# A gated state-space block with a BitNet feed-forward on one core: seven roundings move from GpSimd to VectorE, with a new order of all four queues

## The chip, the cores and the metric

One core of a Trainium2 chip. The time is the device time of one execution in microseconds (us). In the profile PE is TensorE (PEld its weight load), DVE VectorE, ACT ScalarE, POOL GpSimd, SP the engine that issues DMAs.

## The reference

Four batches (B = 4) of 256 tokens with 256 channels. What is computed:

```
z = layernorm(x); h = ctx @ in_proj.T; u = silu(causal conv, 4 taps, of h)
dt_lo, Bm, Cm = u @ x_proj.T            (8, 16 and 16 rows)
delta = softplus(dt_proj @ dt_lo + b);  A = -exp(A_log)
state = state * exp(delta * A) + (delta * u) * Bm    (over 256 steps, 16 states)
y = (sum over states of state * Cm + D * u) * silu(z)
x = x + tanh(g_xattn) * y
n = layernorm(x)
gate, up = act_quant(n) @ weight_quant(w_gate).T, the same with w_up     (256 -> 1024)
i = silu(gate) * up
x = x + tanh(g_ffn) * act_quant(fwht(i)) @ weight_quant(w_down).T        (1024 -> 256)

act_quant(v) = clip(round(v * s), -128, 127) / s,  s = 128 / max|v| of the token
weight_quant(w): w / mean|w| rounded and clipped to -1, 0, 1
fwht: normalized fast Walsh-Hadamard transform over the 1024 channels
```

## The kernel before

Each engine has a list of pieces, written out by hand in the order in which it works them off; between engines stand semaphores alone. A piece waits for its inputs at its head, and whatever is behind it in the same list waits too. Since all four batches are in flight at once, the place of a piece in its list decides much.

The state-space part of a batch f is cut into eight steps of two states; step g = 8f + j. For each: `decays(g)` (ScalarE: four exponentials), `drives(g)` (GpSimd: four products, token on the partition), `drive_rows(g, h)` (TensorE: transposes into PSUM, one bank for each half h), `scan(g, 0)` and `scan(g, 1)` (VectorE: the recurrence), `C_rows(g)` (TensorE), `times_C(g)` (VectorE), `accumulate(g)` (TensorE: sum over the states, transposed back). Rings tie them: decays(g) wait for scan(g-4), drives(g) for drive_rows(g-4), drive_rows(g, h) for scan(g-1, h). The drives of steps 0 and 1 are made by VectorE.

Ahead of it, for each batch: in_proj, silu_u, x_dbl, dt_rows, high_pieces and split (the rows of B and C in bf16 pieces), dt_proj, softplus with softplus_tail on GpSimd, du_T and copy_duT.

Behind it, for each batch f: residual, stats2 (VectorE), rstd2 (ScalarE), second_rstd (GpSimd, eight instructions of one column), second_norm (ScalarE), token_scale (VectorE), scale_tokens (ScalarE: times the scale, plus a magic number), then the **token rounding** (take the magic number off, min with 127, into bf16), tokens_T (TensorE), tokens_out. For each half of the tokens t: gate, silu_gate, up, gate_times_up (VectorE), three fold stages of two instructions each (GpSimd for batches 0 to 2, VectorE's fold_last for batch 3), inter_T, inter_out, hadamard_mm, absmax2 (VectorE), quant_down (ScalarE), the **down rounding** of a 128 x 1024 tile, q2_T, q2_out, down, result (VectorE) and the store. The intermediate lies in `wnat`, the rounded down tile in `wq`, what quant_down writes in `ctxs`.

The two roundings are one instruction each, `tensor_scalar(..., MAGIC + QB - 1, MAGIC, min, subtract)`. In the kernel before GpSimd makes them for tokens of batches 0, 1, 2 (`round_tokens_early`, L1294) and for down tiles (0,0), (0,1), (1,0), (1,1) (`round_down_early`, L1298); VectorE makes those of tokens of batch 3 (L1593) and of down tiles (2,0) to (3,1) (L1632). quant_down waits for the down rounding before it, since both use `ctxs`. gate(f, 0) waits for quant_down(f-1, 1), whose bank it takes.

At the front, ctx_out copies the transposed context of batches 1 to 3 that in_proj(1) needs; weight_abs, weight_sum, weight_means, weight_scale, weight_round, weight_T and weight_out make the ternary weights, spread over batches 0 and 1.

Of the kernel before, what the change touches and what calls it, by code (L numbers as in the profile page):

```python
# [17 lines left out]
LC = L // P  # L18
# [34 lines left out]
def gated_ssm_ffn(nc, x, ctx_1024, g_xattn, g_ffn, in_proj_w, conv_w, conv_b, x_proj_w, dt_proj_w, dt_proj_b,  # L53
                  A_log, D, w_gate, w_up, w_down, ident, hadamard, out):
    stack = ExitStack()
    with stack:
# [3 lines left out]
        def sem(name):  # L60
# [146 lines left out]
        dve_stat2, act_r2, rounded, pe_qT, dve_qT, pe_gate, pe_up, act_sg, dve_mul, act_qT, act_q2T = (  # L207
            sem(n) for n in ("dve_stat2", "act_r2", "rounded", "pe_qT", "dve_qT", "pe_gate", "pe_up", "act_sg", "dve_mul",
                          "act_qT", "act_q2T"))
        pool_fold, pe_tp, act_tp, pe_h, dve_sc, act_tq, rounded_down, pe_q2T, dve_q2T, pe_dn, dve_out = (  # L210
            sem(n) for n in ("pool_fold", "pe_tp", "act_tp", "pe_h", "dve_sc", "act_tq", "rounded_down", "pe_q2T", "dve_q2T",
# [117 lines left out]
        def _(pe):  # L329
# [220 lines left out]
            def tokens_T(f):  # L550

                pe.wait_ge(rounded, f + 1)
# [86 lines left out]
            def q2_T(f, t):  # L639
                pe.wait_ge(rounded_down, LC * f + t + 1)  # L640
# [56 lines left out]
            setup_late()  # L697
# [3 lines left out]
            B_rows(0)  # L701
            in_proj(1, 0)
            du_T(0)
            B_rows(1)
            C_rows(0)
            in_proj(1, 1)
            x_dbl(1)
            drive_rows(2, 0)
            C_rows(1)
            drive_rows(2, 1)  # L710
            dt_proj(1)
            drive_rows(3, 0)
            accumulate(0)
            drive_rows(3, 1)
            C_rows(2)
            drive_rows(4, 0)
            gate_T(0)
            accumulate(1)
            C_rows(3)
            drive_rows(4, 1)  # L720
            drive_rows(5, 0)
            in_proj(2, 0)
            drive_rows(5, 1)
            C_rows(4)
            weight_sum()
            accumulate(2)
            drive_rows(6, 0)
            C_rows(5)
            accumulate(3)
            drive_rows(6, 1)  # L730
            du_T(1)
            accumulate(4)
            in_proj(2, 1)
            C_rows(6)
            weight_T(0)
            drive_rows(7, 0)
            drive_rows(7, 1)
            x_dbl(2)
            drive_rows(8, 0)
            weight_T(1)  # L740
            accumulate(5)
            drive_rows(8, 1)
            accumulate(6)
            C_rows(7)
            drive_rows(9, 0)
            drive_rows(9, 1)
            C_rows(8)
            dt_proj(2)
            accumulate(7)
            drive_rows(10, 0)  # L750
            gate_T(1)
            C_rows(9)
            drive_rows(10, 1)
            weight_T(2)
            drive_rows(11, 0)
            accumulate(8)
            in_proj(3, 0)
            drive_rows(11, 1)
            accumulate(9)
            C_rows(10)  # L760
            drive_rows(12, 0)
            in_proj(3, 1)
            drive_rows(12, 1)
            accumulate(10)
            weight_T(3)
            weight_T(4)
            du_T(2)
            C_rows(11)
            drive_rows(13, 0)
            weight_T(5)  # L770
            x_dbl(3)
            C_rows(12)
            drive_rows(13, 1)
            tokens_T(0)
            accumulate(11)
            gate(0, 0)
            drive_rows(14, 0)
            drive_rows(14, 1)
            C_rows(13)
            gate(0, 1)  # L780
            drive_rows(15, 0)
            drive_rows(15, 1)
            up(0, 0)
            C_rows(14)
            up(0, 1)
            drive_rows(16, 0)
            drive_rows(16, 1)
            accumulate(12)
            C_rows(15)
            drive_rows(17, 0)  # L790
            accumulate(13)
            drive_rows(17, 1)
            accumulate(14)
            dt_proj(3)
            drive_rows(18, 0)
            C_rows(16)
            accumulate(15)
            C_rows(17)
            drive_rows(18, 1)
            accumulate(16)  # L800
            inter_T(0, 0)
            drive_rows(19, 0)
            C_rows(18)
            drive_rows(19, 1)
            drive_rows(20, 0)
            hadamard_mm(0, 0)
            drive_rows(20, 1)
            accumulate(17)
            inter_T(0, 1)
            drive_rows(21, 0)  # L810
            C_rows(19)
            gate_T(2)
            C_rows(20)
            drive_rows(21, 1)
            hadamard_mm(0, 1)
            accumulate(18)
            drive_rows(22, 0)
            drive_rows(22, 1)
            q2_T(0, 0)
            C_rows(21)  # L820
            tokens_T(1)
            accumulate(19)
            du_T(3)
            gate(1, 0)
            drive_rows(23, 0)
            drive_rows(23, 1)
            gate(1, 1)
            accumulate(20)
            drive_rows(24, 0)
            up(1, 0)  # L830
            drive_rows(24, 1)
            C_rows(22)
            accumulate(21)
            down(0, 0)
            accumulate(22)
            q2_T(0, 1)
            C_rows(23)
            drive_rows(25, 0)
            up(1, 1)
            drive_rows(25, 1)  # L840
            accumulate(23)
            gate_T(3)
            C_rows(24)
            down(0, 1)
            drive_rows(26, 0)
            C_rows(25)
            drive_rows(26, 1)
            drive_rows(27, 0)
            inter_T(1, 0)
            hadamard_mm(1, 0)  # L850
            drive_rows(27, 1)
            C_rows(26)
            accumulate(24)
            inter_T(1, 1)
            drive_rows(28, 0)
            accumulate(25)
            hadamard_mm(1, 1)
            q2_T(1, 0)
            accumulate(26)
            C_rows(27)  # L860
            drive_rows(28, 1)
# [1016 lines left out]
```

## Time and profile before

| what | us |
|---|---|
| median of 3 runs | 239.27 (238.29 to 240.78) |
| the profiled execution | 238.49 |
| its span in the trace | 236.4 |
| busy PE / DVE / ACT / POOL | 177.0 / 185.4 / 165.5 / 168.6 |

The span is from the first to the last instruction in the trace; the time of an execution has some us around it. Busy times are sums over the span, and no engine is busy throughout; what bounds a stretch has to be read from that stretch.

### The profile page before, as it was taken

The numbers are of one execution on the slowest core, as the hardware profiler recorded it, in microseconds if no ns is written. First come the engines' busy times: TensorE is split into PE (matmuls) and PEld (weight loads), VectorE is DVE, ScalarE is ACT, GpSimd is POOL, SyncE is SP. The second block draws the span as 40 slices with busy tenths as digits, with TensorE's granted clock in tenths as the row PEclk, the third lists the DMA queues.
The fourth block names the chain that finished last, engine by engine and source line by source line (L and its number), as shares of the span: only waits on it lengthen the run. The fifth ranks groups of instructions, "written<-read, shape, count | busy, mean of one in ns | idle before, by whom it ended". The sixth has DMA issues, their size and how long they took to land.

```text
span 236.4 us, 3708 instructions
## 1 busy us (share of the span) xinstructions
PE 177.0 (75%) x1216; PEld 144.1 (61%) x1216; DVE 185.4 (78%) x270; ACT 165.5 (70%) x285; POOL 168.6 (71%) x262
## 2 busy tenths in 40 slices
PE   3876859988987977788778599956746987575864
PEld 2545637977866966476677467745633776433752
DVE  3518986799999996999978946997668885579962
ACT  2499999996999983999956479968445614733230
POOL 1003079996799999999999999999999999500000
PEclk9985575599999999999979979999999999998895
DMA  3795000000000000000000000000000000000001
GB/s 65 224 348 217 1 1 0 4 0 0 3 0 3 0 0 4 0 0 1 3 1 0 0 0 3 22 25 1 0 0 3 24 22 3 0 22 0 3 22 44
DMA packets 8148, 6.33 MB, mean 27 GB/s; under 512 B 2202, under 2 KB 7874, under 8 KB 8130
## 3 DMA queue, kind: packets, MB, share of 16 engines
q1 hardware_dynamic: 7154, 6.02, 8.0%
q10 hardware_dynamic: 976, 0.09, 0.3%
q8 instruction: 10, 0.16, 0.3%
q14 instruction: 8, 0.07, 0.1%
HBM read 5.05 MB, written 1.05 MB: 26 GB/s over the span
## 4 chain that ended last, share of the span: by engine, by line
POOL 41%; ACT 21%; PE 15%; issue 9%; DVE 8%; DMA 3%; SPq 1%; POOLq 0%; DVEq 0%; ACTq 0%
POOL driveT L1276 11%; POOL wnat L1340 9%; POOL wnat L1341 9%; ACT decay L983 7%; POOL wq L1298 5%; DMA ctxs<-in_ctx_dram 3%; PE PY L468 2%; PE GP L598 2%; POOL q L1294 2%; DVE wnat L1604 2%; DVE wnat L1615 2%; ACT wq L1098 2%; DVE wnat L1614 1%; PE X L497 1%; PE BC L407 1%
## 5 line engine op out<-in xcount | busy, mean ns | idle before, releaser
L1276 POOL TENSOR_SCALAR driveT<-duT,BT 128x256 f32<-128x256 f32 x120 | 56.9, 500 | 13.7 <-ACT duT L1000 10.9
L983 ACT ACTIVATE decay<-delta,zero_c,aneg 128x255 f32<-128x255 f32 x128 | 64.9, 588 | 0.8 <-DVE state L1478 0.7
L1478 DVE TENSOR_TENSOR_SCAN state<-decay,BC 128x512 f32<-128x512 f32 x30 | 36.4, 1213 | 9.8 <-issue 6.9
L1478 DVE TENSOR_TENSOR_SCAN state<-decay,UP 128x512 f32<-128x512 f32 x30 | 36.1, 1203 | 5.7 <-issue 3.3
L1555 DVE TENSOR_TENSOR prod<-state,BC 128x1024 f32<-128x1024 f32 x32 | 38.3, 1198 | 1.1 <-DVE state L1478 0.8
L468 PE MATMUL PY<-id,prod 128*128 128x128 f32 x256 | 35.5, 284 | 1.4 <-DVE prod L1555 0.9
L468 PEld LDWEIGHTS PY<-id,prod 128*128 128x128 f32 x256 | 30.5, 147 | 3.0 <-DVE prod L1555 1.6
L1340 POOL TENSOR_TENSOR wnat<-wnat 128x512 f32<-128x512 f32 x18 | 22.9, 1274 | 0.9 <-DVE wnat L1604 0.2
L1341 POOL TENSOR_TENSOR wnat<-wnat 128x512 f32<-128x512 f32 x18 | 22.9, 1274 | 0.0
L1102 ACT COPY hT<-GP 128x1024 f32<-128x1024 f32 x8 | 8.1, 1008 | 21.2 <-PE GP L616 21.2
L407 PE MATMUL BC<-id,driveT 128*128 128x128 f32 x120 | 19.8, 291 | 3.2 <-POOL driveT L1276 2.2
L407 PE MATMUL UP<-id,driveT 128*128 128x128 f32 x120 | 19.3, 286 | 0.8 <-DVE state L1478 0.7
L407 PEld LDWEIGHTS BC<-id,driveT 128*128 128x128 f32 x120 | 14.8, 150 | 6.4 <-POOL driveT L1276 2.7
L598 PE MATMUL GP<-wT,qT 128*128 128x512 bf16 x56 | 14.6, 383 | 5.0 <-ACT wq L1098 2.8
L407 PEld LDWEIGHTS UP<-id,driveT 128*128 128x128 f32 x120 | 15.3, 149 | 2.9 <-issue 1.7
L452 PE MATMUL BC<-bc,sel 96*128 96x256 bf16 x64 | 13.0, 285 | 5.3 <-DVE prod L1555 5.3
L616 PE MATMUL GP<-id,wnat 128*128 128x128 f32 x64 | 9.0, 286 | 7.6 <-POOL wnat L1341 3.4
L1305 POOL TENSOR_TENSOR rest<-raw,high 64x256 f32<-64x256 f32 x4 | 2.7, 665 | 16.7 <-ACT raw L1041 16.7
L1298 POOL TENSOR_SCALAR wq<-ctxs 128x1024 bf16<-128x1024 f32 x4 | 14.6, 3639 | 0.0
L616 PEld LDWEIGHTS GP<-id,wnat 128*128 128x128 f32 x64 | 7.3, 145 | 8.9 <-POOL wnat L1341 3.8
L1098 ACT ACTIVATE wq<-GP,zero_c,gs 128x1024 f32<-128x1024 f32 x7 | 8.4, 1205 | 5.9 <-PE GP L598 5.9
L1604 DVE SCALAR_TENSOR_TENSOR wnat<-GP,us,wq 128x1024 f32<-128x1024 f32 x7 | 8.9, 1271 | 3.6 <-issue 2.9
(210 smaller groups left out, 390.5 us busy)
## 6 DMA issues: line engine op xcount, KB each, us to landing
wnat<-in_L_ffn_w_gate_dram SPq DMA_DIRECT2D x1, 1024.0 KB, 9.4
xs<-in_x_dram SPq DMA_DIRECT2D x1, 1024.0 KB, 11.8
wnat<-in_L_ffn_w_up_dram SPq DMA_DIRECT2D x1, 1024.0 KB, 11.9
wnat<-in_L_ffn_w_down_dram SPq DMA_DIRECT2D x1, 1024.0 KB, 11.3
out_dram<-ot SPq DMA_DIRECT2D x8, 128.0 KB, 1.7
ctxs<-in_ctx_dram SPq DMA_DIRECT2D x1, 384.0 KB, 6.9
ctxs<-in_ctx_dram SPq DMA_DIRECT2D x1, 128.0 KB, 2.7
inw<-n_L_xattn_in_proj_w_dram SPq DMA_DIRECT2D x1, 128.0 KB, 2.7
```

Source lines behind the costliest of these rows:

```text
L407: last = nc.tensor.transpose(drive_bank(h)[:, L * n + P * c:L * n + P * (c + 1)], driveT[:, m % RING, c, n, P * h:P * (h + 1)], id32[:])
L468: last = nc.tensor.matmul(PY[:, E * c + P * h:E * c + P * (h + 1)], prod[:, g % RING, h, n, P * c:P * (c + 1)], id32[:], is_transpose=True ...
L598: last = nc.tensor.matmul(ffn_bank(f, t)[:, 512 * i:512 * (i + 1)], qT[:, h, P * t:P * (t + 1)], w[:, h, 512 * i:512 * (i + 1)], start=(h ...
L616: last = nc.tensor.transpose(GP[:, P * a:P * (a + 1)], fold[:, t, P * a:P * (a + 1)], id32[:])
L983: last = nc.scalar.activation(decay[:, m % RING, h, n, 1:L], delta[:, b % 2, h, 1:L], ACT.Exp, bias=zero_c[:], scale=aneg[:, h, NB * j + n ...
L1276: last = nc.gpsimd.tensor_scalar(driveT[:, m % RING, c, n], duT[:, b % 2, c], BT[:, b % 2, c, NB * j + n:NB * j + n + 1], 1.0, ALU.mult, A ...
L1298: nc.gpsimd.tensor_scalar(q2[:, t], tq, MAGIC + QB - 1, MAGIC, ALU.min, ALU.subtract).then_inc(rounded_down, 1)
L1340: nc.gpsimd.tensor_tensor(dst[:, :, 0, :], src[:, :, 0, :], src[:, :, 1, :], ALU.add)
L1341: nc.gpsimd.tensor_tensor(dst[:, :, 1, :], src[:, :, 0, :], src[:, :, 1, :], ALU.subtract).then_inc(done, 1)
L1478: nc.vector.tensor_tensor_scan(state[:, g % STATES, h].rearrange("p n l -> p (n l)"), decay[:, g % RING, h].rearrange("p n l -> p (n l)"), ...
L1555: nc.vector.tensor_tensor(prod[:, g % RING].rearrange("p h n l -> p h (n l)"), state[:, g % STATES].rearrange("p h n l -> p h (n l)"), PC. ...
L1604: nc.vector.scalar_tensor_tensor(out=inter[:, t], in0=ffn_bank(f, t)[:], scalar=us[:, t:t + 1], in1=sg[:, t], op0=ALU.mult, op1=ALU.mult). ...
```

## The change

All seven roundings that GpSimd made go to VectorE; `round_tokens_early` and `round_down_early` are gone, and the semaphores are renamed. VectorE's list has `round_tokens(0)` before times_C(12), `round_down(0, 0)` before scan(20, 0), `round_tokens(1)` between scan(21, 0) and result(0, 0), `round_down(0, 1)` before times_C(20), `round_down(1, 0)` before times_C(26), `round_tokens(2)` after scan(28, 0), `round_down(1, 1)` after scan(30, 0). The lists of all four engines are put in a new order throughout; no piece but the roundings changes its engine, and no instruction changes.

The core of the diff (order lists shortened to the places that matter here):

```diff
@@ GpSimd
-            def round_tokens_early(f):
-                pool.wait_ge(act_xr, f + 1)
-                nc.gpsimd.tensor_scalar(q[:], xn[:], MAGIC + QB - 1, MAGIC, ALU.min, ALU.subtract).then_inc(rounded, 1)
-
-            def round_down_early(f, t):
-                pool.wait_ge(act_tq, LC * f + t + 1)
-                nc.gpsimd.tensor_scalar(q2[:, t], tq, MAGIC + QB - 1, MAGIC, ALU.min, ALU.subtract).then_inc(rounded_down, 1)
...
             token_factors(0)
-            drives(14)
-            drives(15)
-            round_tokens_early(0)
-            drives(16)
             drives(17)
...
             drives(22)
-            round_down_early(0, 0)
-            softplus_tail(3, pool, nc.gpsimd, pool_front_link, 1)
-            round_tokens_early(1)
-            token_factors(1)
             softplus_tail(3, pool, nc.gpsimd, pool_front_link, 2)
             drives(23)
             drives(24)
             drives(25)
-            round_down_early(0, 1)
             drives(26)
             fold_tile(1, 0, 0)
             fold_tile(1, 0, 1)
+            drives(27)
             fold_tile(1, 0, 2)
-            drives(27)
             fold_tile(1, 1, 0)
             fold_tile(1, 1, 1)
-            drives(28)
             fold_tile(1, 1, 2)
             second_rstd(2)
-            round_down_early(1, 0)
+            drives(28)
+            token_factors(2)
             drives(29)
-            round_tokens_early(2)
-            token_factors(2)
             drives(30)
             drives(31)
-            round_down_early(1, 1)
             fold_tile(2, 0, 0)
@@ VectorE
             def round_tokens(f):
                 dve.wait_ge(act_xr, f + 1)
-                nc.vector.tensor_scalar(q[:], xn[:], MAGIC + QB - 1, MAGIC, ALU.min, ALU.subtract).then_inc(rounded, 1)
+                nc.vector.tensor_scalar(q[:], xn[:], MAGIC + QB - 1, MAGIC, ALU.min, ALU.subtract).then_inc(dve_q, 1)
...
+            round_down(0, 0)
             scan(20, 0)
             scan(20, 1)
             times_C(19)
             token_scale(1, dve_ln_link)
             scan(21, 0)
+            round_tokens(1)
+            result(0, 0)
+            absmax2(0, 1)
             scan(21, 1)
+            round_down(0, 1)
             times_C(20)
-            absmax2(0, 1)
...
             scan(27, 0)
             scan(27, 1)
+            round_down(1, 0)
             times_C(26)
+            token_scale(2, dve_ln_link)
             scan(28, 0)
-            token_scale(2, dve_ln_link)
+            round_tokens(2)
             absmax2(1, 1)
...
             scan(30, 0)
+            round_down(1, 1)
             gate_times_up(2, 0)
-            result(1, 0)
             scan(30, 1)
-            gate_times_up(2, 1)
             times_C(29)
             scan(31, 0)
             scan(31, 1)
+            result(1, 0)
             times_C(30)
+            gate_times_up(2, 1)
+            times_C(31)
             result(1, 1)
-            times_C(31)
...
             tokens_out(3)
+            absmax2(2, 1)
             q2_out(2, 0)
-            absmax2(2, 1)
+            gate_times_up(3, 0)
+            round_down(2, 1)
+            fold_last(0)
+            gate_times_up(3, 1)
             result(2, 0)
-            gate_times_up(3, 0)
-            fold_last(0)
-            round_down(2, 1)
-            gate_times_up(3, 1)
             fold_last(1)
@@ ScalarE
+            silu_u(0)
             inw_out()
-            tanh_gates()
-            silu_u(0)
-            ctx_out()
             for_exp()
             dt_rows(0)
+            high_pieces(0)
             weight_abs(0)
+            softplus(0)
             exp_A()
-            high_pieces(0)
-            softplus(0)
             copy_B(0)
+            ctx_out()
             copy_BT(0)
...
             decays(3)
-            copy_BT(1)
-            high_pieces(1)
+            softplus(1)
             decays(4)
-            softplus(1)
+            gate_out(0)
+            weight_abs(2)
             decays(5)
-            weight_abs(2)
-            gate_out(0)
             decays(6)
...
+            q2_out_early(1, 0)
+            tokens_out_early(2)
             quant_down(1, 1)
-            tokens_out_early(2)
             silu_gate(2, 0)
             silu_gate(2, 1)
-            q2_out_early(1, 0)
@@ TensorE
             gate(3, 0)
+            gate(3, 1)
+            up(3, 0)
             down(2, 0)
-            up(3, 0)
-            gate(3, 1)
             up(3, 1)
```

## Rows read from the trace of the kernel before

**Rows 1.** Busy time of each engine by stretch (x instructions), granted clock, DMA:

```profile
core 0: us, PE busy (x) PEld busy (x) DVE busy (x) ACT busy (x) POOL busy (x), PEclk, DMA share, GB/s
30.00:60.00 30.00, 25.31 (x145) 22.14 (x146) 24.30 (x25) 27.70 (x53) 25.44 (x37) 0.77 0.01 2
60.00:90.00 30.00, 25.46 (x210) 22.46 (x209) 29.67 (x37) 27.75 (x56) 28.29 (x54) 1.00 0.00 1
90.00:185.00 95.00, 70.79 (x536) 57.77 (x536) 77.60 (x94) 70.02 (x116) 93.20 (x129) 0.96 0.01 4
185.00:203.00 18.00, 13.89 (x117) 11.88 (x115) 13.10 (x20) 6.92 (x10) 17.06 (x21) 1.00 0.05 16
203.00:236.40 33.40, 20.84 (x148) 15.07 (x147) 23.71 (x44) 11.17 (x12) 1.76 (x5) 0.86 0.05 16
```

**Rows 2.** Chain of waits that ended last, share of the span by engine:

```profile
POOL 41%; ACT 21%; PE 15%; issue 9%; DVE 8%; DMA 3%; SPq 1%; POOLq 0%; DVEq 0%; ACTq 0%
```

**Rows 3.** Groups of instructions by shape, GpSimd: the roundings:

```profile
L1298 POOL TENSOR_SCALAR wq<-ctxs 128x1024 bf16<-128x1024 f32 x4 | 14.6, 3639 | 0.0
...
L1294 POOL TENSOR_SCALAR q<-xn 128x512 bf16<-128x512 f32 x3 | 5.8, 1935 | 0.0
```

**Rows 4.** Groups by shape, VectorE: the same roundings in the tail:

```profile
L1632 DVE TENSOR_SCALAR wq<-ctxs 128x1024 bf16<-128x1024 f32 x4 | 2.8, 692 | 1.3 <-ACT ctxs L1108 1.3
...
L1593 DVE TENSOR_SCALAR q<-xn 128x512 bf16<-128x512 f32 x1 | 0.4, 428 | 0.5 <-ACT xn L1092 0.5
```

**Rows 5.** Timeline, GpSimd (start, duration): pairs beside roundings, one alone:

```profile
77.27 1.60 POOL L1320 TENSOR_SCALAR nt<-ve,r 128x1 f32<-128x1 f32 x2
...
123.51 0.50 POOL L1320 TENSOR_SCALAR nt<-ve,r 128x1 f32<-128x1 f32 x2
...
205.21 1.04 POOL L1287 TENSOR_SCALAR gs<-amax,wmean 128x1 f32<-128x1 f32 x2 [2.19 <-DVE amax L1585]
206.21 0.74 POOL L1289 TENSOR_SCALAR us<-amax,wmean 128x1 f32<-128x1 f32 x2
```

**Rows 6.** Timeline, VectorE, at the same times:

```profile
77.28 1.22 DVE L1656 TENSOR_SCALAR wq<-wnat 128x2048 bf16<-128x2048 f32 x1
...
205.27 0.69 DVE L1632 TENSOR_SCALAR wq<-ctxs 128x1024 bf16<-128x1024 f32 x1
206.47 0.43 DVE L1593 TENSOR_SCALAR q<-xn 128x512 bf16<-128x512 f32 x1 [0.51 <-ACT xn L1092]
```

**Rows 7.** Timeline, GpSimd: drives of batch 3, folds of batch 2:

```profile
137.29 5.64 POOL L1276 TENSOR_SCALAR driveT<-duT,BT 128x256 f32<-128x256 f32 x12
...
185.28 1.27 POOL L1340 TENSOR_TENSOR wnat<-wnat 128x512 f32<-128x512 f32 x1 [0.20 <-DVE wnat L1604]
...
199.29 1.27 POOL L1341 TENSOR_TENSOR wnat<-wnat 128x512 f32<-128x512 f32 x1
```

**Rows 8.** Timeline, VectorE: times_C(6), times_C(14), gaps, gate_times_up(1,0), gate_times_up(2,0):

```profile
63.26 1.19 DVE L1555 TENSOR_TENSOR prod<-state,BC 128x1024 f32<-128x1024 f32 x1
...
101.74 1.20 DVE L1555 TENSOR_TENSOR prod<-state,BC 128x1024 f32<-128x1024 f32 x1
...
140.02 1.22 DVE L1478 TENSOR_TENSOR_SCAN state<-decay,BC 128x512 f32<-128x512 f32 x1 [3.32 <-issue]
...
144.32 1.28 DVE L1604 SCALAR_TENSOR_TENSOR wnat<-GP,us,wq 128x1024 f32<-128x1024 f32 x1 [1.98 <-issue]
...
183.91 1.28 DVE L1604 SCALAR_TENSOR_TENSOR wnat<-GP,us,wq 128x1024 f32<-128x1024 f32 x1 [0.68 <-PE GP L598]
```

**Rows 9.** Timeline, ScalarE: decays(5) and second_norm(3):

```profile
45.03 2.06 ACT L983 ACTIVATE decay<-delta,zero_c,aneg 128x255 f32<-128x255 f32 x4
...
203.05 1.09 ACT L1084 ACTIVATE xn<-x,mr,rn 128x256 f32<-128x256 f32 x2 [0.29 <-POOL mr L1326]
```

**Rows 10.** Groups by shape, ScalarE: the decays:

```profile
L983 ACT ACTIVATE decay<-delta,zero_c,aneg 128x255 f32<-128x255 f32 x128 | 64.9, 588 | 0.8 <-DVE state L1478 0.7
```

More of the change, by code:

```diff
@@ L770, in _ @@
+            accumulate(11)
+            C_rows(12)
+            drive_rows(13, 1)
+            du_T(2)
             weight_T(5)
             x_dbl(3)
[L772 to L776, printed above, removed]
             drive_rows(14, 0)
             drive_rows(14, 1)
+            tokens_T(0)
+            gate(0, 0)
             C_rows(13)
+            drive_rows(15, 0)
             gate(0, 1)
[L781 removed]
@@ L798, in _ @@
+            dt_proj(3)
+            drive_rows(16, 1)
+            C_rows(15)
+            accumulate(14)
+            drive_rows(17, 0)
+            drive_rows(17, 1)
+            accumulate(15)
+            C_rows(16)
+            drive_rows(18, 0)
+            up(0, 1)
+            drive_rows(18, 1)
+            inter_T(0, 0)
             C_rows(17)
-            drive_rows(18, 1)
+            hadamard_mm(0, 0)
+            drive_rows(19, 0)
+            gate_T(2)
+            drive_rows(19, 1)
@@ L813, in _ @@
+            drive_rows(21, 1)
+            tokens_T(1)
+            drive_rows(22, 0)
+            accumulate(19)
             C_rows(20)
[L814 to L817, printed above, removed]
             drive_rows(22, 1)
-            q2_T(0, 0)
+            gate(1, 0)
+            accumulate(20)
+            du_T(3)
+            drive_rows(23, 0)
             C_rows(21)
-            tokens_T(1)
-            accumulate(19)
-            du_T(3)
@@ L824, in _ @@
-            gate(1, 0)
-            drive_rows(23, 0)
+            gate(1, 1)
             drive_rows(23, 1)
-            gate(1, 1)
-            accumulate(20)
+            up(1, 0)
+            accumulate(21)
+            C_rows(22)
             drive_rows(24, 0)
-            up(1, 0)
+            C_rows(23)
             drive_rows(24, 1)
-            C_rows(22)
-            accumulate(21)
-            down(0, 0)
+            q2_T(0, 1)
+            drive_rows(25, 0)
             accumulate(22)
-            q2_T(0, 1)
@@ L837, in _ @@
-            C_rows(23)
-            drive_rows(25, 0)
+            drive_rows(25, 1)
+            C_rows(24)
             up(1, 1)
-            drive_rows(25, 1)
+            drive_rows(26, 0)
+            down(0, 1)
             accumulate(23)
-            gate_T(3)
[L843 to L847, printed above, removed]
+            inter_T(1, 0)
+            drive_rows(26, 1)
+            C_rows(25)
+            hadamard_mm(1, 0)
@@ L1202, in _ @@
             decays(18)
+            softplus(3)
             decays(19)
+            inter_out(0, 0)
             decays(20)
+            gate_out(2)
+            quant_down(0, 0)
+            rstd2(1)
             decays(21)
-            softplus(3)
             decays(22)
-            inter_out(0, 0)
-            decays(23)
-            rstd2(1)
-            quant_down(0, 0)
+            q2_out_early(0, 0)
             second_norm(1)
@@ L1214, in _ @@
             scale_tokens(1)
-            gate_out(2)
+            decays(23)
+            tokens_out_early(1)
+            quant_down(0, 1)
             for_silu()
             silu_z(3)
-            tokens_out_early(1)
-            quant_down(0, 1)
+            silu_gate(1, 0)
             copy_duT(3)
-            silu_gate(1, 0)
-            q2_out_early(0, 0)
             silu_gate(1, 1)
@@ L1731, in _ @@
             times_C(10)
+            scan(12, 0)
             weight_out(2)
+            scan(12, 1)
+            times_C(11)
             token_scale(0, dve_ln_link)
-            scan(12, 0)
-            scan(12, 1)
             weight_out(3)
-            weight_out(4)
-            times_C(11)
-            weight_out(5)
             scan(13, 0)
             scan(13, 1)
+            weight_out(4)
+            weight_out(5)
+            round_tokens(0)
             times_C(12)
```

238 lines of the change are left out of this document (116 added, 122 removed).

## Prediction

> **What bounds the kernel now.** I read the busy time by stretch first, because averages hide the stages. Four stretches differ [rows 1]. In 30 to 60 us no engine is full, ScalarE is nearest (27.70 of 30). In 60 to 90 VectorE is full (29.67 of 30). In 90 to 185 GpSimd is (93.20 of 95), while VectorE has 17.4 us free, ScalarE 25.0, TensorE 24.2. From 203 on GpSimd does 1.76 us and the last batch runs as one dependent chain of 33.4 us. Then the chain of waits: 41% of it lies on GpSimd, ScalarE is next with 21% [rows 2]. Then GpSimd's own groups by tile: the roundings are seven instructions, four of 3639 ns for the down tiles (L1298) and three of 1935 ns for tokens (L1294), 14.6 + 5.8 = 20.4 us [rows 3], all inside 90 to 185. So what bounds the middle is GpSimd, with these in its queue; there the end is set by gate_times_up(2,0) on VectorE (183.91), behind which GpSimd folds without a gap (185.28 to 200.56) before it can make the statistics of the last batch [rows 7, 8].
>
> **The roundings.** VectorE makes the same two instructions for the last tiles already: 692 ns and 428 ns [rows 4]. GpSimd loses 20.4 us, VectorE gains 4 x 0.69 + 3 x 0.43 = 4.1 us. Two bounds of the gain follow: GpSimd alone could give 20.4; VectorE has 17.4 us free in 90 to 185 and takes 4.1, so at most 13.3 us can go before VectorE is full there. From below: zero, if each rounding on VectorE waits as long as it saves.
>
> Each rounding also takes its wait with it. On VectorE scans and times_C stand behind it, and ScalarE (next decays), TensorE (drive_rows wait for scans) and GpSimd (drives wait for drive_rows) behind those. The wait is for ScalarE (scale_tokens, quant_down), whose own queue has groups of four decays in it at 588 ns each [rows 10], 2.1 us as pitched.
>
> **The order.** I laid the new lists of the four busy engines end to end with durations of the old trace, each piece starting at the latest of its waits. The landmarks:
> - Front. ctx_out now follows softplus(0), so in_proj(1) and with it x_dbl(1) come later; softplus(1), gate_out(0) and weight_abs(2) stand before decays(5), which begins near 50.1 instead of 45.03 [rows 9]. It costs little, since VectorE's queue was later than that already: I get the end of times_C(6) near 64.8 plus a weight_out that was inside the old figure, against 63.26 + 1.19 = 64.5 [rows 8], so 1.0 us late. Drives of GpSimd begin 2 us earlier, but wait for duT(1), near 61.9, as before. The full stretch 60 to 90 hands the 1.0 us on. Round_tokens(0) waits for scale_tokens(0), which ends near 91.9, VectorE being there at 92.3: no wait. The gaps of 90 to 103 take the lateness up: times_C(14) ends near 102.8, against 101.74 + 1.20 = 102.9 [rows 8]. Gain so far 0. Bounds: 5 us worse if decays(5) shifts the scans in full, 2 us better if the earlier drives are passed on.
> - Batch 1. Its tokens are rounded near 128.7 rather than on GpSimd at 135.1. What is late next is quant_down(0,1) near 132.1 (gate(1,0) waits for its bank), behind absmax2(0,1), and then the copy of duT(3), near 136.5; in the old trace the last eight of the twelve drives at 137.29 stood behind it [rows 7]. The idle 3.32 and 1.98 us of VectorE at 140 and 144 [rows 8] shrink: gate_times_up(1,0) starts near 140.0, old 144.32. Gain 4.3.
> - Batch 2. GpSimd now runs from 141.2 through six fold stages (twelve instructions of 1.27), drives(27) and second_rstd(2) without a rounding, to 161.1. Then come second_norm(2), token_scale(2), round_tokens(2) near 165.3, absmax2(1,1), quant_down(1,1) near 168.8, gate(2,0), silu, gate(2,1), silu, up(2,0); gate_times_up(2,0) starts near 175.0, old 183.91. Gain 8.9. GpSimd stands idle near 170 to 176: it has stopped being the bound there, and the loop VectorE, ScalarE, TensorE is.
> - Folds of batch 2. Twelve instructions, 15.3 us as before (185.28 to 199.29 + 1.27) [rows 7], gate_times_up(2,1) being in time near 183.8; then second_rstd(3). second_norm(3) near 193.7, old 203.05 [rows 9]. Gain 9.4.
> - Tail. The same chain of 33.4 us [rows 1]. gate(3,1) ahead of up(3,0) and an early absmax2(2,1) hide nothing that was late, but result(2,0) leaves a gap of VectorE and now stands between gate_times_up(3,1) and fold_last(1): its 0.4 us and some placing, +0.4. Bounds -1 and +1.5.
>
> Sum of the lists: 236.4 - 9.4 + 0.4 = 227.4 us of span.
>
> **A cost the lists don't have.** Some of GpSimd's instructions stretch when VectorE rounds. The pair L1320 takes 0.50 us at 123.51 but 1.60 at 77.27, exactly while a weight rounding of 1.22 runs on VectorE (77.28). At 205.21 the pair gs takes 1.04 instead of 0.50, beside round_down(2,0) at 205.27; at 206.21 the pair us takes 0.74, beside q at 206.47 [rows 5, 6]. So GpSimd stands still for 0.54 us at a down rounding and 0.24 at a token rounding; 4 x 0.54 + 3 x 0.24 = 2.9 us for the seven, bounded by 0 and by the 4.1 us that they run. Half of GpSimd's time in question is on the path (it idles near 136 and 170), so +1.5. Span 228.9.
> The Trainium skill (SBUF - State Buffer, "Who interferes with whom") says that VectorE and GpSimd share one pair of ports by an exclusive lock, and that a VectorE instruction in a two-port mode shuts GpSimd out while it runs; the trace agrees, with the 1.60 against 0.50 us. By its full lock the cost would be the upper bound, 4.1, and not 2.9.
>
> **The time.** The profiled execution took 238.49 us with a span of 236.4, so 2.1 us lie around it: 228.9 + 2.1 = 231.0. The median of the runs, 239.27, is 0.8 above that execution: 231.8.
>
> **Rivals.**
> - *VectorE waits for GpSimd.* The stand-still could also go the other way: a rounding that finds a fold instruction of 1.27 us running waits for its end, half of it on average, 7 x 0.64 = 4.4 us, and the waiting is on VectorE, which is then the engine of the loop. With the other 1.4 us of the stand-still also on the path: 231.8 + 5.8 = 237.6. For it: fold instructions fill much of 141 to 161. Against it: no rounding or weight rounding of the old trace shows a wait before it; but none met a long instruction of GpSimd as it began. The page named above says that whichever instruction starts first keeps the pair, which is this rival's rule.
> - *The roundings are queued too early on VectorE.* Place: round_down(0,0), round_tokens(1), round_down(0,1), round_tokens(2). If ScalarE's piece before them is one group of decays late, scans stand for 2.07 us, the decays behind wait for the scans, and nothing catches up. All seven: 231.8 + 14.5 = 246.3. It turns slower by over 1% from (241.7 - 231.8) / 7 = 1.4 us of waiting per rounding. For it: at round_down(0,1) my lists leave no slack (quant_down ends 132.1, VectorE is there at 132.1). Against it: in the others VectorE comes 0.5 to 3 us after the data.
> - *The full bound.* My list is too strict in the loop (old waits hold some overlap that I charge twice), and VectorE fills up in 90 to 185: 239.3 - 13.3 = 226.0. For it: the earlier drives. Against it: four engines in a loop have never all been full in the old trace.
>
> **Chances.** Forecast 231.8 (228.5 to 235.5): 0.68. VectorE waits for GpSimd, 237.6: 0.13. Too early, 246.3: 0.08. Full bound, 226: 0.11. The range for 8 in 10 is 226.5 to 238.0, the second rival in, the third mostly out. A run of this kernel can tell about 1% (its three times span 238.3 to 240.8). Faster by over 1% (under 236.9): the forecast, the full bound and a small part of the first rival, 0.81; within 1%: 0.11; slower: 0.08.
>
> **What would show it.** In the changed profile: no L1298 or L1294 on GpSimd, seven more short ones on VectorE with less than 0.5 us of idle before each; GpSimd idle for some us before the folds of batch 2; gate_times_up(1,0) near 140 and gate_times_up(2,0) near 175; the tail still 33 us. Pairs such as gs that stretch beside a rounding confirm the stand-still. Wrong would be: times_C(14) well after 103 (the front costs), gate_times_up(2,0) after 181 (the gain is lost in the loop), or idle of over 1.4 us before each rounding.

## The result and the profile after

Median after 235.21 us (234.16 to 236.20, four runs), before on the same chip 239.17 (238.29 to 240.78): ratio 0.985 [0.980, 0.989]. A second measurement on another chip gave 0.982 [0.978, 0.985]. So the change is 1.5 to 1.8% faster, some 4 us, where 231.8, a gain of 7.5, was forecast; the range 226.5 to 238.0 holds the time. The profiled execution took 235.95 us, with a span of 234.2 and a mean granted clock of 0.934.

Busy time by stretch, the changed kernel:

```profile
core 0: us, PE busy (x) PEld busy (x) DVE busy (x) ACT busy (x) POOL busy (x), PEclk, DMA share, GB/s
30.00:60.00 30.00, 23.15 (x123) 19.43 (x124) 23.45 (x24) 26.55 (x50) 26.27 (x36) 0.77 0.00 1
60.00:90.00 30.00, 27.89 (x220) 24.74 (x218) 29.75 (x36) 26.30 (x56) 25.91 (x47) 0.94 0.00 1
90.00:185.00 95.00, 73.93 (x581) 60.56 (x580) 89.12 (x109) 75.52 (x124) 81.50 (x134) 0.98 0.01 4
```

Against [rows 1], GpSimd has fallen from 93.20 to 81.50 us of 95 and VectorE has risen from 77.60 to 89.12: no engine is full in the middle any more. The chain of waits says the same; before it was 41% GpSimd and 8% VectorE [rows 2]:

```profile
POOL 33%; ACT 22%; PE 22%; DVE 12%; issue 9%; DMA 1%; SPq 0%; POOLq 0%; ACTq 0%; DVEq 0%
```

The landmarks of the prediction, from the timelines (us). "After" is the first profile of the changed kernel and "after, again" a second one, from experiment 6; "drive_rows late" is experiment 10, the changed kernel with one piece of TensorE moved back:

| landmark | before | forecast | after | after, again | drive_rows late |
|---|---|---|---|---|---|
| end of times_C(6) | 64.5 | 64.8 | 66.1 | 65.6 | 62.8 |
| end of times_C(14) | 102.9 | 102.8 | 105.8 | 104.5 | 101.7 |
| gate_times_up(1,0) starts | 144.3 | 140.0 | 143.7 | 142.7 | 139.6 |
| gate_times_up(2,0) starts | 183.9 | 175.0 | 179.8 | 178.8 | 176.1 |
| second_norm(3) starts | 203.1 | 193.7 | 198.9 | 197.9 | 195.2 |
| from there to the end of the span | 33.4 | 33.7 | 35.3 | 33.4 | 34.2 |

Stretch by stretch the span changed by +2.9 (front), -3.5 (to gate_times_up(1,0)), -3.5 (to gate_times_up(2,0)), 0 (folds) and +2.0 (tail) in the first profile, 2.2 us less together; in the second by +1.5, -3.1, -3.5, 0 and 0, 5.1 less. The medians differ by 4: the first profiled execution of after was 0.7 us slower than its median, that of before 0.7 to 0.8 faster.

VectorE, changed kernel, the rows that answer to [rows 8], and second_norm(3) of ScalarE, to [rows 9]:

```profile
104.62 1.21 DVE L1540 TENSOR_TENSOR prod<-state,BC 128x1024 f32<-128x1024 f32 x1
...
143.71 1.26 DVE L1589 SCALAR_TENSOR_TENSOR wnat<-GP,us,wq 128x1024 f32<-128x1024 f32 x1
...
179.78 1.28 DVE L1589 SCALAR_TENSOR_TENSOR wnat<-GP,us,wq 128x1024 f32<-128x1024 f32 x1 [0.58 <-issue]
```

```profile
198.90 1.09 ACT L1084 ACTIVATE xn<-x,mr,rn 128x256 f32<-128x256 f32 x2
```

**The front.** Changed kernel, timelines of GpSimd, TensorE, ScalarE and VectorE in turn:

```profile
28.87 9.53 POOL L1276 TENSOR_SCALAR driveT<-duT,BT 128x256 f32<-128x256 f32 x12 [10.60 <-ACT duT L1000]
```

```profile
33.93 1.12 PE L407 MATMUL BC<-id,driveT 128*128 128x128 f32 x4 [4.78 <-POOL driveT L1276]
34.84 1.91 PE L513 MATMUL GP<-u,xpwT 128*104 128x256 f32 x4
36.54 1.73 PE L415 MATMUL GP<-xpwT,u 128*128 128x16 f32 x8
```

```profile
38.31 0.36 ACT L1046 COPY dtlo<-GP 8x256 f32<-8x256 f32 x1 [3.21 <-PE GP L415]
...
38.78 2.07 ACT L983 ACTIVATE decay<-delta,zero_c,aneg 128x255 f32<-128x255 f32 x4
```

```profile
40.88 1.22 DVE L1463 TENSOR_TENSOR_SCAN state<-decay,BC 128x512 f32<-128x512 f32 x1 [4.82 <-ACT decay L983]
```

drive_rows(2, 0) (L407) now stands ahead of x_dbl(1) (L513, L415) and waits 4.78 us for GpSimd, whose first twelve drives take 9.53 us: 794 ns each, where later ones take 460 (1.84 for four). x_dbl(1) waits behind it though it needs nothing of GpSimd. On ScalarE dt_rows(1) (L1046) waits 3.21 us for x_dbl(1), with the decays of scan(2, 0) queued behind it, so that scan comes at 40.88; in the kernel before it came at 37.32. Two moves make this together. In the old list of ScalarE decays(2) stood ahead of dt_rows(1) and did not wait for x_dbl(1); ScalarE, kernel before:

```profile
34.02 2.07 ACT L983 ACTIVATE decay<-delta,zero_c,aneg 128x255 f32<-128x255 f32 x4
...
36.32 0.36 ACT L1046 COPY dtlo<-GP 8x256 f32<-8x256 f32 x1 [0.23 <-PE GP L415]
```

**The roundings.** VectorE, changed kernel, groups by shape, then the three token roundings and the one down tile that stretched:

```profile
L1617 DVE TENSOR_SCALAR wq<-ctxs 128x1024 bf16<-128x1024 f32 x8 | 5.8, 729 | 1.4 <-ACT ctxs L1108 1.3
...
L1578 DVE TENSOR_SCALAR q<-xn 128x512 bf16<-128x512 f32 x4 | 2.6, 654 | 0.5 <-ACT xn L1092 0.5
```

```profile
93.59 0.67 DVE L1578 TENSOR_SCALAR q<-xn 128x512 bf16<-128x512 f32 x1
...
131.30 0.94 DVE L1578 TENSOR_SCALAR q<-xn 128x512 bf16<-128x512 f32 x1
...
135.65 1.05 DVE L1617 TENSOR_SCALAR wq<-ctxs 128x1024 bf16<-128x1024 f32 x1
...
169.68 0.58 DVE L1578 TENSOR_SCALAR q<-xn 128x512 bf16<-128x512 f32 x1
```

None of the seven has idle time in front: the 1.4 and 0.5 us of waiting in the groups lie in the tail. But four last longer than the 0.43 and 0.69 us of [rows 4], by 0.24, 0.51, 0.36 and 0.15 us: 1.3 us. On GpSimd, changed kernel, two of the stretched pieces beside them:

```profile
124.84 0.89 POOL L1309 TENSOR_SCALAR ve<-mv,r 128x1 f32<-128x1 f32 x2
...
131.93 0.67 POOL L1287 TENSOR_SCALAR gs<-amax,wmean 128x1 f32<-128x1 f32 x2
```

Alone such a pair takes 0.50; with a third pair (1.03) and the drives beside a rounding (four take 2.30 or 2.00 where they take 1.84 alone) it is about 1.7 us for GpSimd.

**The fold engine.** GpSimd before the folds of batch 2, changed kernel. It stands idle for 6.47 us there, from 174.7 to 181.2; the prediction had said 170 to 176:

```profile
181.15 1.27 POOL L1332 TENSOR_TENSOR wnat<-wnat 128x512 f32<-128x512 f32 x1 [6.47 <-DVE wnat L1589]
```

### The profile page after: what moved, and what is told of

Same layout as the page of the kernel before. It is cut to its first block, busy times and chain, and to the rows that moved or that the text cites. A ratio compares the mean times of both kernels' runs of the same rounds, so it can differ in the third digit from the quotient of the medians.

```text
span 234.2 us, 3710 instructions
## 1 busy us (share of the span) xinstructions
PE 177.2 (76%) x1216; PEld 143.5 (61%) x1216; DVE 190.6 (81%) x277; ACT 165.2 (71%) x285; POOL 152.6 (65%) x255
## 4 chain that ended last, share of the span: by engine, by line
POOL 33%; ACT 22%; PE 22%; DVE 12%; issue 9%; DMA 1%; SPq 0%; POOLq 0%; ACTq 0%; DVEq 0%
POOL driveT L1276 11%; POOL wnat L1332 6%; POOL wnat L1333 6%; ACT decay L983 6%; PE GP L598 3%; PE PY L468 2%; PE BC L407 2%; PE UP L407 2%; ACT wq L965 2%; DVE wnat L1589 2%; DVE wnat L1600 2%; ACT wq L1098 2%; ACT ctxs L1108 2%; DVE wnat L1599 1%; POOL spa L287 1%
## 5 line engine op out<-in xcount | busy, mean ns | idle before, releaser
L1276 POOL TENSOR_SCALAR driveT<-duT,BT 128x256 f32<-128x256 f32 x120 | 59.7, 516 | 15.5 <-ACT duT L1000 10.6
L468 PE MATMUL PY<-id,prod 128*128 128x128 f32 x256 | 34.2, 278 | 0.9 <-DVE prod L1540 0.8
L468 PEld LDWEIGHTS PY<-id,prod 128*128 128x128 f32 x256 | 29.5, 143 | 3.0 <-DVE prod L1540 2.1
L407 PE MATMUL BC<-id,driveT 128*128 128x128 f32 x120 | 20.2, 296 | 10.0 <-POOL driveT L1276 8.2
L407 PEld LDWEIGHTS BC<-id,driveT 128*128 128x128 f32 x120 | 15.1, 152 | 12.5 <-POOL driveT L1276 9.2
L407 PE MATMUL UP<-id,driveT 128*128 128x128 f32 x120 | 20.1, 294 | 0.8 <-DVE state L1463 0.8
L598 PE MATMUL GP<-wT,qT 128*128 128x512 bf16 x56 | 15.8, 408 | 5.1 <-ACT wq L1098 2.3
L452 PE MATMUL BC<-bc,sel 96*128 96x256 bf16 x64 | 12.7, 280 | 7.7 <-DVE prod L1540 7.7
L407 PEld LDWEIGHTS UP<-id,driveT 128*128 128x128 f32 x120 | 15.5, 152 | 3.0 <-issue 1.7
L598 PEld LDWEIGHTS GP<-wT,qT 128*128 128x128 bf16 x56 | 5.1, 102 | 11.6 <-issue 4.8
L452 PEld LDWEIGHTS BC<-bc,sel 96*128 96x128 bf16 x64 | 5.7, 102 | 10.4 <-issue 9.9
```

Of the source, the lines that this page charges most:

```text
L407: last = nc.tensor.transpose(drive_bank(h)[:, L * n + P * c:L * n + P * (c + 1)], driveT[:, m % RING, c, n, P * h:P * (h + 1)], id32[:])
L452: last = nc.tensor.matmul(PC[:, L * n:L * (n + 1)], row_pick(DS + NB * j + n), bc3[:, b, :], start=True, stop=True)
L468: last = nc.tensor.matmul(PY[:, E * c + P * h:E * c + P * (h + 1)], prod[:, g % RING, h, n, P * c:P * (c + 1)], id32[:], is_transpose=True ...
L598: last = nc.tensor.matmul(ffn_bank(f, t)[:, 512 * i:512 * (i + 1)], qT[:, h, P * t:P * (t + 1)], w[:, h, 512 * i:512 * (i + 1)], start=(h ...
L1276: last = nc.gpsimd.tensor_scalar(driveT[:, m % RING, c, n], duT[:, b % 2, c], BT[:, b % 2, c, NB * j + n:NB * j + n + 1], 1.0, ALU.mult, A ...
```

## The experiments

Each ratio is to the kernel before on the same chip. The granted clock differs between executions of one kernel, so landmarks are compared over several profiles, and a difference of medians below 1% is no more than a hint.

**1 and 2. Roundings without the order, order without the roundings.** The first is the kernel before with round_tokens and round_down on VectorE at places of the old list:

```diff
 GpSimd:  -round_tokens_early(0..2)  -round_down_early(0,0) (0,1) (1,0) (1,1)
 VectorE: +round_tokens(0)  before times_C(12)   +round_down(0,0) before times_C(19)
          +round_tokens(1)  before times_C(20)   +round_down(0,1) before times_C(21)
          +round_down(1,0)  before times_C(26)   +round_tokens(2) before scan(28,1)
          +round_down(1,1)  before times_C(27)
```

> The old order of all queues; only the seven roundings go to VectorE, each in front of the times_C or scan at which ScalarE's data is ready by the old trace. Theory A (the roundings bring the 7 us that the middle gains, the new order only costs at both ends): about 232 us, faster than the changed kernel. Rival B (the new order is what makes room, the roundings alone only swap GpSimd's time for VectorE's waits): 238 to 239 us.

The second is the changed kernel with all seven back on GpSimd, near their old places.

> The new order of all queues with the seven roundings left on GpSimd, each behind the piece of GpSimd's new list by which its data is ready. Theory A: the order alone costs 3 us at the front and 2 in the tail, with GpSimd as full as before, so 243 to 245 us. Rival B (the order makes room): 235 to 237 us.

Measured: 0.978 [0.973, 0.982] and 1.036 [1.032, 1.040]. In the old order the move gains 2.2%, 5.4 us. The new order with the roundings on GpSimd is 8.7 us slower than before, and 0.053 (12.7 us) slower than with them on VectorE. So the gain is the engine's, and the new order isn't a gain by itself: with the roundings on VectorE it adds nothing that can be told (0.983 against 0.978, medians of 235.2 and 234.3 against 234.7), and it needs them there. The landmarks say the same. From the end of times_C(14) to gate_times_up(2,0) the kernel before takes 81.0 us; with the roundings on VectorE it is 74.6 in the old order and 74.0 and 74.3 in the new one. What the new order does with them on GpSimd; GpSimd, then VectorE:

```profile
128.99 3.63 POOL L1298 TENSOR_SCALAR wq<-ctxs 128x1024 bf16<-128x1024 f32 x1
132.60 1.84 POOL L1276 TENSOR_SCALAR driveT<-duT,BT 128x256 f32<-128x256 f32 x4
```

```profile
134.66 1.22 DVE L1478 TENSOR_TENSOR_SCAN state<-decay,UP 128x512 f32<-128x512 f32 x1 [6.92 <-issue]
```

The drives stand behind the rounding, their transposes behind the drives, and VectorE is idle for 6.92 us until its scan, which starts as the last of these transposes ends.

**3 and 4. Which roundings.** The changed kernel with the token roundings alone, or the down roundings alone, back on GpSimd:

```diff
 tokens:  GpSimd +round_tokens_early(0..2) behind token_factors(0..2)
          VectorE -round_tokens(0..2)
 down:    GpSimd +round_down_early behind second_rstd(1), drives(23), second_rstd(2), drives(31)
          VectorE -round_down(0,0) (0,1) (1,0) (1,1)
```

> The changed kernel with the roundings of tokens of batches 0 to 2 back on GpSimd; those of the down tiles stay on VectorE. All seven back cost 0.0531 x 240 = 12.3 us in the new order. If that is paid by the time on GpSimd (3 x 1.94 = 5.8 us against 4 x 3.65 = 14.6 us), this kernel is 3.5 us slower than the changed one. Rival (the tokens stand on the way into each batch's feed-forward part and are waited for at once, while the down tiles have time): 6 us or more here, and little for the down tiles.

> The changed kernel with the four roundings of down tiles back on GpSimd; those of tokens stay on VectorE. By the time on GpSimd this is 8.8 us slower than the changed kernel; by the rival, that the tokens are what is waited for, 6 us or less.

Measured: 1.002 [0.997, 1.006] and 1.018 [1.011, 1.025], so 4.5 and 8.4 us slower than the changed kernel's 0.983. Together 12.8, which is the 12.7 of all seven. GpSimd takes on 5.8 us for the tokens and VectorE loses 1.3: 4.5 net, paid in full. For the down tiles it is 14.6 - 2.8 = 11.8 net, of which 8.4 are paid. Both lie near what the time on GpSimd gives (3.5 and 8.8), and the rival's "6 us or more" for tokens did not come. Per microsecond of work the tokens seem to cost more, but with intervals of 1 to 2 us on each figure that is not shown.

**5. Does VectorE pay for them?** The changed kernel with each of the seven made twice:

```diff
+                if f < B - 1:
+                    nc.vector.tensor_scalar(q_twin, xn[:], MAGIC + QB - 1, MAGIC, ALU.min, ALU.subtract)
...
+                if f < B - 2:
+                    nc.vector.tensor_scalar(q2_twin[:], tq, MAGIC + QB - 1, MAGIC, ALU.min, ALU.subtract)
```

> The changed kernel with each of the seven roundings that are made between and beside the batches (three of tokens, four of down tiles) made twice on VectorE, the first copy into a tile that nobody reads. That adds 3 x 428 + 4 x 692 = 4.1 us of VectorE work, and some microsecond in which the two engines hold each other up. Theory (VectorE has room in the loops, so the change gained what it took off GpSimd and paid almost nothing for it): at most 2 us slower than the changed kernel. Rival (VectorE has become the engine that ends the loops, and the moved work is paid in full there): 4 to 6 us slower.

Measured: 0.981 [0.976, 0.985], the changed kernel 0.982 and 0.985. 4.1 us more of VectorE's work cost nothing that can be measured (the intervals leave room for 1 to 1.5 us); from times_C(12) to gate_times_up(2,0) the loop takes 85.2 us against 84.4. VectorE, busy for 94% of the stretch from 90 to 185, is not what sets its time. What sets it now is not shown: no engine is full, and the chain of waits is spread over GpSimd, TensorE and ScalarE. The twins also show what the stretching is:

```profile
92.79 0.68 DVE L1581 TENSOR_SCALAR q_twin<-xn 128x512 bf16<-128x512 f32 x1
93.39 0.41 DVE L1582 TENSOR_SCALAR q<-xn 128x512 bf16<-128x512 f32 x1
...
130.19 0.92 DVE L1581 TENSOR_SCALAR q_twin<-xn 128x512 bf16<-128x512 f32 x1
131.03 0.42 DVE L1582 TENSOR_SCALAR q<-xn 128x512 bf16<-128x512 f32 x1
...
134.63 1.16 DVE L1622 TENSOR_SCALAR q_twin<-ctxs 128x1024 bf16<-128x1024 f32 x1
135.71 0.68 DVE L1623 TENSOR_SCALAR wq<-ctxs 128x1024 bf16<-128x1024 f32 x1
```

Three of the seven first roundings are long (0.68, 0.92, 1.16); the second, the same instruction on the same data right behind it, is never longer than 0.42 or 0.69, though GpSimd had an instruction under way beside six of the seven. So it isn't a slower rate: the first waits at its start, inside its recorded time, and the second does not. In the two longest an instruction of 1.27 us was running on GpSimd as the rounding began (129.56 to 130.83 and 133.97 to 135.24); taken back from its end by its usual 0.42 or 0.69, each rounding begins at 130.69 and 135.10, within 0.15 us of the end of that instruction.

**6. The changed kernel again.**

> The changed kernel itself, on the chip of the next runs, to have them beside it: 1.5% faster than the kernel before, as in the first comparison.

Measured: 0.982 [0.978, 0.985]. The profiled execution has a span of 231.3 and a clock of 0.956, against 234.2 and 0.934 of the first. Its tail, from second_norm(3) to the end of the last result instruction, takes 31.1 us; in the first it took 33.1, and in the kernel before 31.2. The stretches in question, first profile of the changed kernel:

```profile
198.90:208.30 9.40, 7.60 (x43) 4.29 (x44) 4.76 (x13) 6.05 (x8) 1.74 (x4) 0.82 0.00 0
208.30:234.00 25.70, 15.27 (x107) 11.94 (x105) 18.87 (x32) 5.00 (x5) 0.00 (x0) 0.87 0.06 21
```

and the second profile of the same kernel:

```profile
197.90:206.20 8.30, 6.07 (x43) 3.85 (x44) 4.72 (x12) 5.65 (x8) 1.74 (x4) 1.00 0.00 0
206.20:231.00 24.80, 14.67 (x108) 12.11 (x105) 19.08 (x32) 5.35 (x5) 0.00 (x0) 0.86 0.07 22
```

The same pieces from second_norm(3) to gate_times_up(3,0) take 9.40 us at a granted clock of 0.82 and 8.30 at 1.00. So the 2.0 us that the tail seemed to lose belong to that execution and not to the change: 1.1 of them to this stretch, 0.9 to the one behind it, where the granted clocks are nearly the same.

**7 and 8. The tail.** The changed kernel with the old tail on TensorE, ScalarE and VectorE (q2_T(3,1) is behind down(3,0) there too); and with q2_T(3,1) alone put back behind down(3,0):

```diff
 TensorE, all of the tail     |  TensorE, one piece
-            gate(3, 1)        | -            q2_T(3, 1)
-            up(3, 0)          |              down(3, 0)
             down(2, 0)        | +            q2_T(3, 1)
+            up(3, 0)
+            gate(3, 1)
```

> The changed kernel with the old order of the tail on all queues (from gate(3, 0) on TensorE, silu_gate(3, 0) on ScalarE, tokens_out(3) on VectorE). Theory A (the new tail order costs what the trace of after shows over my forecast: 35.3 us from second_norm(3) to the end against 33.4): 2 us faster than the changed kernel, about 233.2 us. Rival (the tail is longer because TensorE's granted clock is lower there, not by the order): 0 to 0.8 us faster, 234.4 to 235.2.

> The changed kernel with one piece of TensorE moved: q2_T(3, 1) behind down(3, 0), as it was. down(3, 0) then runs while TensorE would wait for the last rounding. Theory: 0.8 us faster than the changed kernel, the distance that its trace shows from the last q2_out to the last down over the old one (1.5 against 0.7 us). Rival (no cost there): 0.

Measured: 0.972 [0.968, 0.976] and 0.979 [0.975, 0.982]. Tails by the measure of experiment 6: eight profiles with the new tail took 33.1 and seven times 31.0 to 32.0 us, mean 31.6; five with the old one (the kernel before among them) 31.2 to 31.6, mean 31.4; with down(3,0) first 31.7. So the tail's order costs some 0.2 us, too little against the spread to be called shown. The run times look larger. With the old tail the median is 233.50 against 234.29 of the changed kernel, 0.8 us; the ratio is 1.0 to 1.3% better, mostly because the kernel before was 1.4 us slower on that chip (240.02 against 238.62), and which of the two to trust is open, since the profiles show none of it (spans of 232.0 and 231.3). With down(3,0) first the median is 0.85 us lower, as the theory said, but the intervals overlap and the profile's tail is not shorter.

**9 and 10. The front.** The changed kernel with the old front on all four queues; and with one piece alone moved:

```diff
 TensorE
-            drive_rows(2, 0)
             x_dbl(1)
+            drive_rows(2, 0)
```

> The changed kernel with the old order of the front on all four queues (VectorE up to times_C(6), GpSimd up to weight_scale(1), TensorE up to x_dbl(2), ScalarE up to the third exponential table). Theory A (the front makes times_C(14) 2.9 us late and the rest hands this on): 2.9 us faster than the changed kernel, about 232.3 us. Rival (a later stretch waits for something else and takes the lateness up): no difference, 235.2 us.

> The changed kernel with one piece of TensorE moved: drive_rows(2, 0) behind x_dbl(1), as it was. Theory A1 (the front is late because x_dbl(1) stands behind drive_rows(2, 0), which waits 4.8 us for GpSimd's first products): x_dbl(1) starts 1 to 2 us earlier and most of that reaches the end, 1 to 2 us faster than the changed kernel. Rival (ctx_out, softplus(1) and weight_abs(2) ahead of the decays are the cause): within 0.5 us of the changed kernel.

Measured: 0.971 [0.967, 0.975] and 0.975 [0.969, 0.980]. TensorE, then VectorE, with drive_rows late:

```profile
32.80 1.11 PE L513 MATMUL GP<-u,xpwT 128*104 128x256 f32 x4 [2.73 <-ACT u L1017]
33.74 0.96 PE L415 MATMUL GP<-xpwT,u 128*128 128x16 f32 x8
34.55 0.63 PE L407 MATMUL BC<-id,driveT 128*128 128x128 f32 x4
```

```profile
37.60 1.22 DVE L1463 TENSOR_TENSOR_SCAN state<-decay,BC 128x512 f32<-128x512 f32 x1 [1.62 <-ACT decay L983]
```

Both expectations of a gain are met in kind: against the changed kernel's medians of 235.21 and 234.29 these are 233.22 and 233.72. The wait for GpSimd is gone, since the drives are there by the time x_dbl(1) is done. scan(2, 0) starts at 37.60; in eight profiles of kernels with the full new front it starts between 40.09 and 40.95. times_C(6) ends at 62.8, against 65.3 to 66.2 in eight, and times_C(14) at 101.7, against 104.2 to 105.8 in the six of them with all roundings or all tokens on VectorE; the span is 229.4. From the start of scan(2, 0) to the end of times_C(6) it is 25.2 us here and in all eight (25.21 to 25.25), so how late times_C(6) is follows from that scan alone. And the lead is kept: against the second profile of the changed kernel it is 2.8 us at times_C(6), 2.8 at times_C(14), 2.7 at gate_times_up(2,0) and 2.7 at second_norm(3).

Not all of the lead is the order's, though. TensorE's granted clock was also higher in this execution while x_dbl(1) ran; changed kernel, first profile, then drive_rows late:

```profile
34.00:37.00 3.00, 3.00 (x11) 2.52 (x12) 2.06 (x2) 1.10 (x1) 3.00 (x5) 0.50 0.00 0
```

```profile
34.00:37.00 3.00, 2.06 (x18) 1.68 (x18) 1.98 (x2) 2.96 (x7) 3.00 (x6) 1.00 0.00 0
```

x_dbl(1) starts 2.0 us earlier (32.80 against 34.84) and takes 1.9 us instead of 3.4. With 3.4 it would have ended at 36.2 and held dt_rows(1), which began at 35.0, up by 1.2 us. So by this estimate some 2 of the 3.3 us at scan(2, 0) are the order's and 1.2 the clock's; whether the order also helps the clock is open. The runs fit that: two took 230.4 and 231.2 us at a mean granted clock of 0.97, four 233.7 to 234.7 at 0.90 to 0.93, the median is 0.6 us below the changed kernel's, and the intervals overlap.

With the old front as a whole times_C(6) ends at 64.5, but times_C(14) only at 104.5; the granted clock was low in 92 to 96 us of that profile:

```profile
92.00:96.00 4.00, 3.32 (x17) 2.45 (x18) 3.11 (x3) 1.46 (x4) 4.00 (x11) 0.51 0.01 2
```

gate(0,0) took 1.89 us there and 1.04 at full clock. The first profile of the changed kernel has such a stretch as well (gate(0,0) took 1.53; 0.89 is the mean of 90 to 106 us), the second has not. Like with like, at a granted clock of 1.00 in 90 to 106 us, times_C(14) ends at 104.2 to 104.9 in five profiles with the new front and at 102.2 and 103.0 in the two with the old one (experiments 11 and 12). The order of the front so costs about 2 us there.

**11 and 12. Both ends old, new middle; and in it one piece more.** The second moves C_rows(13) ahead of gate(0,0), since in the first profile of the changed kernel times_C(13) waited 1.27 us behind it.

```diff
 TensorE
             tokens_T(0)
+            C_rows(13)
             gate(0, 0)
-            C_rows(13)
```

> The changed kernel with the old front and the old tail together, so the new order stands in the middle alone. Theory A (both ends cost, each for itself): the two gains of about 3 us add up, 230.5 us where the changed kernel takes 236. Rival (the two variants gained mostly by the same thing, TensorE's granted clock, which was at its lower level less often in them): no more than 1 us better than either alone, 232.5 us.

> The kernel with the old front and tail and the new middle, and in it C_rows(13) put ahead of gate(0,0) on TensorE, so that it runs while gate(0,0) waits for qT. Theory (times_C(13) comes 1.3 us late because C_rows(13) stands behind that wait, and what is lost there stays lost): 1 to 2 us faster than the same kernel without this, which had a ratio of 0.9721. Rival (the loops behind are set by GpSimd or ScalarE, and the wait is taken up): no difference.

Measured: 0.972 [0.968, 0.976] (median 231.83) and 0.965 [0.960, 0.970] (median 231.69), the fastest two of the study; both beat the kernel before and the changed one. On the same chip the old ends are worth 2.5 us (231.83 against 234.29). The first expectation is not settled: by ratio both ends together are no better than either alone (0.971 and 0.972), which is what the rival said, by medians 1.4 to 1.7 us better; and the clocks of the six runs (0.92 to 0.94) are no higher than the changed kernel's (0.93 to 0.96), so the rival's reason does not show. Against the old order with the same roundings (experiment 1, 234.70 and 0.978) the new middle gains 2.9 us in medians, 0.6% and 1.3% by ratio, of which only the second is clear of the intervals. In the profiles it does not show behind times_C(14): 74.0 and 74.5 us to gate_times_up(2,0), against 74.6.

The second is no better than the first. VectorE, ends old:

```profile
94.87 1.22 DVE L1540 TENSOR_TENSOR prod<-state,BC 128x1024 f32<-128x1024 f32 x1 [0.26 <-DVE state L1463]
...
97.90 1.22 DVE L1463 TENSOR_TENSOR_SCAN state<-decay,UP 128x512 f32<-128x512 f32 x1 [0.68 <-issue]
```

and with C_rows(13) moved:

```profile
95.31 1.20 DVE L1540 TENSOR_TENSOR prod<-state,BC 128x1024 f32<-128x1024 f32 x1
...
98.69 1.22 DVE L1463 TENSOR_TENSOR_SCAN state<-decay,UP 128x512 f32<-128x512 f32 x1 [1.05 <-issue]
```

times_C(13) no longer waits, and the scan behind it waits 0.4 us longer. From times_C(12) to times_C(14) it is 10.0 us in both; the medians differ by 0.14 us, and the ratios by the kernel before, which was 1.4 us slower on the second chip. The rival was right: no difference. There was also little to win: the wait was 0.26 us with the ends old, and in the changed kernel's second profile too; the 1.27 of the first profile stood behind gate(0,0) at a lower clock.

## Why the prediction was right or wrong

- **What bounds it** was right: seven roundings on GpSimd were the price of the middle. Taking them off gained 5.4 us in the old order and 12.7 in the new one, between its bounds 0 and 13.3.
- **Front: "Gain so far 0" is the step that failed.** times_C(14) was to end at 102.8 and ended at 105.8 and 104.5; "times_C(14) well after 103" was the prediction's own sign that the front costs. Two parts of the step were wrong. times_C(6) ended at 66.1 and 65.6, not at 64.8. I looked at decays(5) and gave it a bound of 5 us, and it was not that: I passed over drive_rows(2, 0), which had moved ahead of x_dbl(1) and waits for drives that take 794 ns each there, and over dt_rows(1), now ahead of decays(2). And "the gaps of 90 to 103 take the lateness up" did not come: at full clock times_C(14) ends 38.9 us behind times_C(6) whether the front is late or early (the second profile and drive_rows late), where I had 38.0, and the lateness goes on to the end. The rest of the 105.8, about 0.8 us, is a stretch of lower granted clock. With drive_rows(2, 0) put back the front ends at 101.7, 1.1 us before my figure, and the later landmarks come within 0.4 to 1.5 us of the forecast, in part by luck of that execution's clock.
- **Batches 1 and 2.** Forecast gains 4.3 and 4.6 us, measured 3.5 and 3.5 (3.1 and 3.5 in the second profile); the folds, 0.5 forecast, gave none. The mechanism is the forecast one: GpSimd runs from drives to folds, then idles for 6.47 us. The loop term was mis-sized by 2.4 us (7.0 for 9.4) and by 2.7 (6.7).
- **The stand-still** was sized 1.5 us on the path. GpSimd lost 1.7 in all and VectorE 1.3. That may be where most of the 2.4 went; it was not measured by itself. With it the miss of the loop is 0.9 to 1.2.
- **Tail: +0.4**, measured +0.2 as a mean of profiles. The +2.0 of the first profile did not come back in the second (0). I had overlooked that q2_T(3,1) moved ahead of down(3,0); put back, it changed nothing that can be told.
- **Rivals.** "VectorE waits for GpSimd" is real in kind (the twins show it) and wrong in size: 1.3 us for seven against my 4.4. Two roundings met an instruction of 1.27 us and waited 0.51 and 0.36, near the half that I had said, but most met none. It is not on the path besides, as 4.1 us of added work on VectorE cost nothing. "Queued too early": no rounding waited. "Full bound": VectorE has 5.9 of 95 us left idle, and still isn't the bound.
- **Sum of spans**: 228.9 forecast. The first profile has 234.2: 2.9 front, 0.9 loop, 1.5 tail, together 5.3. The second has 231.3: 1.5 front, 1.2 loop, -0.4 tail, together 2.4 with rounding. In medians the miss is 3.4 and 2.5 us. That the range held the time is no merit of the mechanism: about half of the forecast gain came.

By the Trainium skill (SBUF - State Buffer, "Who interferes with whom") the shared port pair is held exclusively by one engine at a time. The traces fit it in both directions: pairs of GpSimd grow from 0.50 to 0.89 beside a rounding, and a rounding of VectorE from 0.42 to 0.92 behind an instruction of GpSimd.

## What to carry to other kernels

When one engine is full in the stretch that sets the time and another does the same instruction in a fifth of the time, move it; test whether the receiver pays by doing the moved work twice. When lists are reordered, check each piece that moved ahead of another for what it waits for: one transpose in front of a matmul that needed nothing of GpSimd cost about 2 us by the estimate of experiment 10, where seven moved roundings gained 5.4 in the old order. Don't count on gaps behind a delay to take it up: here they took up nothing. And profile the same kernel twice before explaining a difference of a microsecond.

## What was not expected of the hardware

- The same program drew different granted clocks: spans of 234.2 (0.934) and 231.3 (0.956), with 1.1 us of it in one stretch of nine. With drive_rows late the six runs took 230.4 and 231.2 at clocks of 0.97, and 233.7 to 234.7 at 0.90 to 0.93. A single profile can't settle a difference in the whole time below 3 us in this kernel.
- A rounding that waits for GpSimd shows that as a longer instruction, not as idle time before it: 0.92 us, and 0.42 for its twin right behind.
- GpSimd's first twelve drives took 794 ns each as a mean, later ones 460; in the kernel before the first four took 910. VectorE's first scans run beside them; that these hold them up was argued and not tried.
